# Router on un-normalised rows, with the bias, statistics and slot integers moved to other places in the queues

## What is computed

```python
x = x + xattn(layernorm(x), ctx)            # 16 heads of 16, softmax(q k^T / 4) v, then Wo and bo
xf = layernorm(x).reshape(-1, 256)
logits = xf @ router_w.T + router_b         # 32 experts
e = argmax(logits)
out = x + relu(relu(xf @ w1[e] + b1[e]) @ w2[e] + b2[e])
```

## Time and profile before

| | |
|---|---|
| median of three runs | 1132.77 us (1130.8 to 1137.42) |
| the profiled execution: time, span of its core | 1134.33 us, 1132.5 us |
| PE busy | 1050.1 us, 93% |
| DVE busy | 916.1 us, 81% |
| ACT busy | 825.7 us, 73% |
| POOL busy | 839.3 us, 74% |
| mean granted clock of PE | 0.973 of 2.4 GHz |

### The profile page before, as it was taken

One profiled execution on the slowest core, in us unless ns is written; L12 is line 12 of the kernel. 1 busy time (PEld: TensorE's weight loads), 2 busy tenths in 40 slices (PEclk: granted clock), 3 DMA queues, 4 the chain that ended last, 5 costly groups with the idle time before them and its releaser, 6 DMA issues.

```text
span 1132.5 us, 39071 instructions
## 1 busy us (share of the span) xinstructions
PE 1050.1 (93%) x15015; PEld 877.7 (77%) x15015; DVE 916.1 (81%) x2355; ACT 825.7 (73%) x1892; POOL 839.3 (74%) x1579
## 2 busy tenths in 40 slices
PE   5998999999999999999999999999998369998982
PEld 4887888878888888888888888888886258887872
DVE  4887788888888888888888888888887547776761
ACT  5776787878888888888888888888885236665651
POOL 5436688778878887888888878878866747777776
PEclk9999999999999999999999999999999679999997
DMA  7525222532222222323222222222210366666650
GB/s 234 186 60 130 77 78 77 125 105 77 77 78 82 82 86 78 90 82 104 83 83 77 77 78 77 78 77 78 72 53 22 109 190 200 208 207 210 202 150 12
DMA packets 91164, 120.38 MB, mean 106 GB/s; under 512 B 14105, under 2 KB 73892, under 8 KB 90790
## 3 DMA queue, kind: packets, MB, share of 16 engines
q1 hardware_dynamic: 77159, 84.04, 26.1%
q0 software_dynamic: 13824, 33.85, 8.3%
HBM read 60.61 MB, written 59.31 MB: 106 GB/s over the span
## 4 chain that ended last, share of the span: by engine, by line
PE 80%; DVE 5%; DMA 5%; POOL 4%; issue 3%; ACT 1%; SPq 0%; POOLq 0%; DVEq 0%; ACTq 0%
PE maxima L789 18%; PE pA L849 10%; PE sc L826 10%; PE sc L856 10%; PE sc L796 8%; PE sc L780 5%; PE sc L1036 4%; PE maxima L803 3%; PE maxima L1044 3%; POOL out L431 3%; PE sc L835 2%; DMA arena<-pages 2%; DMA out<-arena 2%; PE sc L1027 2%; PE pA L803 2%
## 5 line engine op out<-in xcount | busy, mean ns | idle before, releaser
L480 ACT ACTIVATE arena<-sc 128x512 f32<-128x512 f32 x512 | 264.4, 603 | 93.3 <-PE sc L835 93.3
L597 DVE TENSOR_REDUCE mx<-maxima 128x4 bf16<-128x512 f32 (+1 forms) x256 | 235.1, 919 | 5.2 <-PE maxima L803 4.0
L431 POOL DMA_INDIRECT out<-arena x160 | 157.6, 985 | 60.3 <-issue 30.8
L396 POOL DMA_INDIRECT pages<-row,slot_i x128 | 130.6, 1020 | 55.4 <-issue 53.4
L826 PE MATMUL sc<-qk 32*128 32x256 f32 x2048 | 152.1, 394 | 0.3 <-DVE xnT L617 0.3
L856 PE MATMUL sc<-wo_s,aT 128*128 128x256 f32 x512 | 132.5, 381 | 7.9 <-ACT arena L480 4.9
L849 PE MATMUL pA<-arena 128*32 128x128 f32 x4096 | 138.4, 276 | 0.0
L622 DVE STREAM_TRANSPOSE tr<-pA 128x512 f32<-128x512 f32 x128 | 90.7, 708 | 43.8 <-PE pA L849 43.4
L557 ACT ACTIVATE arena<-sc 128x256 f32<-128x256 f32 x160 | 61.5, 384 | 79.4 <-PE sc L1027 78.2
L849 PEld LDWEIGHTS pA<-arena 128*32 128x32 f32 x4096 | 107.1, 110 | 10.8 <-issue 5.0
L796 PE MATMUL sc<-wqkv,cHi 128*128 128x256 f32 x512 | 107.3, 302 | 0.0
(11 more groups left out here) (155 smaller groups left out, 2709.8 us busy)
## 6 DMA issues: line engine op xcount, KB each, us to landing
arena<-pages SPq DMA_DIRECT2D x160, 130.0 KB, 3.0
cT<-ctxT SPq DMA_DIRECT2D x64, 256.0 KB, 4.1
xs<-x_in SPq DMA_DIRECT2D x128, 128.0 KB, 3.4
pages<-empty SPq DMA_DIRECT2D x120, 130.0 KB, 3.5
pages<-empty SPq DMA_DIRECT2D x1, 5200.0 KB, 20.0
out<-arena POOLq DMA_INDIRECT x160
w2s<-w SPq DMA_DIRECT2D x1, 2080.0 KB
qk<-w SPq DMA_DIRECT2D x1, 2064.0 KB, 9.9
```

What stands on the lines that cost most here:

```text
L396: pool.indirect_dma_start(pages, bass.IndirectOffsetOnAxis(slot_i[:, q % 2, u:u + 1], 0), row[:, q % 4, u, :], None, bounds_check=last_slo ...
L431: pool.indirect_dma_start(out_rows, bass.IndirectOffsetOnAxis(pr[:, r, COL_TOKEN:COL_TOKEN + 1].bitcast(U32), 0), pr[:, r, 0:D], None, bou ...
L480: act.activation(pt[:, u % 2, g].rearrange("p i k -> p (i k)"), sc[g][:, :], ACT.Exp).then_inc(S["exp_out"], 1)
L597: dve.tensor_reduce(mx[:, :].rearrange("p (g h) -> p g h", h=32)[:, g:g + n, 0:4], src.rearrange("p (g h k) -> p g h k", g=n, h=4), AX.X, ...
```

## The change

The router is applied to the rows as they are. Its weights are centred in the set-up: a product of a constant 1/D matrix with the weights gives their means, and DVE subtracts these (`wr_c`). So the mean of a row drops out, and only its factor is missing; `logits_across` applies it as the per-token scale of four activations of 32 columns, and the router's bias is added by DVE as a new first operation of `best`. `norm2` and `xn2` go, and PE transposes `row` directly, waiting for the residual only. In the queues: on POOL `place(s-3)` stands ahead of `add_bo(s)`, which now waits for the normalise of the last unit of the block before; the slot integers are made by DVE, behind `slot_sum`; on DVE `stats1(.., (3,))` of a block moves from u=3 of one superstep to u=0 of the next; and PE makes seven products of 512 columns between the last slot integers and the first page. The set-up loses the transposed router bias. The diff:

```diff
--- before.py
+++ after.py
@@ -79,18 +79,18 @@
         cst = sb("cst", [C_ALL])
         wqkv = sb("wqkv", [3, 2, 2, D], F32R)
         wo_s = sb("wo_s", [2, D])
-        wr_s = sb("wr_s", [2, E])
+        wr_s, wr_c = sb("wr_s", [2, E]), sb("wr_c", [2, E])
         bq_s, bk_s = sb("bq_s", [2]), sb("bk_s", [2])
         bqm = sb("bqm", [2, 2])
         bv_s, bo_s, rb_s = sb("bv_s", [D]), sb("bo_s", [D]), sb("rb_s", [E])
         bvT = sb("bvT", [2, P])
-        rb4, rbp = sb("rb4", [QB, E]), sb("rbp", [1])
+        rb4 = sb("rb4", [QB, E])
         ident_b, tri_b, ones_b = sb("ident_b", [P], BF16), sb("tri_b", [P], BF16), sb("ones_b", [P], BF16)
         sel_b = sb("sel_b", [4, P], BF16)
         half = sb("half", [QB])
         xs = sb("xs", [4, QB, D])
         row = sb("row", [4, QB, ROW])
-        xn, xn2 = sb("xn", [QB, D]), sb("xn2", [QB, D])
+        xn, sq = sb("xn", [QB, D]), sb("sq", [2, D])
         xnT = sb("xnT", [2, 2, QB * P], F32R)
         xn2T = sb("xn2T", [2, QB * P])
         cT = sb("cT", [2, QB * P])
@@ -144,9 +144,9 @@
 
         names = """ld_c0 ld_c1 ld_cst ld_wk ld_wq ld_wv ld_b ld_wo ld_wr ld_w1 ld_w2 fill fill0 fill1 fill2 fill3
           pool_init dve_init cst_ready mask_ready wk_hi wq_hi wv_hi wk_lo wq_lo wv_lo w2_zero ex_init
-          bvT_done bvT_out bo_done bo_out rbT_done rbp_out rb4_out
+          bvT_done bvT_out bo_done bo_out wr_out rb4_out
           S_done T_done PV_done O_done V_done proj_done mxT_done xnT_done xn2T_done lg_done lgT_done rk_done
-          exp_out V_out proj_out xnT_out xn2T_out lgs_out rk_out xn_out xn2_out
+          exp_out V_out proj_out xnT_out xn2T_out lgs_out rk_out xn_out lb_out
           max_out mxT_out tr_out inv_out nrm_out aT_out x2_out sq_out stat1_out agg1_out xnTl_out
           lg_out top_out eq_out pick_out idx_out hot_out scan_out slot_out
           var1_out pow1_out mr1_out rstd1_out mean2_out sq2_out eps2_out var2_out pow2_out rstd2_out
@@ -352,7 +352,7 @@
                     pool.wait_ge(S["bo_out"], 1)
                 after(pool, "xn_out", 2, q, 1)
                 if q >= 1:
-                    after(pool, "nrm_out", 4, q - 1, 2)
+                    after(pool, "nrm_out", 4, q - 1, 3)
                 pool.tensor_tensor(xs[:, q % 4], xs[:, q % 4], bo_s[:, :].unsqueeze(1).to_broadcast([P, QB, D]),
                                    ALU.add).then_inc(S["xb_out"], 1)
 
@@ -379,12 +379,6 @@
                 pool.tensor_copy(row[:, q % 4, :, COL_EXPERT].bitcast(I32), expert[:, :]).then_inc(S["meta_out"], 1)
                 pool.tensor_scalar(tok[:, :], tok[:, :], float(QB * P), None, ALU.add).then_inc(S["tok_out"], 1)
 
-            def slots_as_integers(q):
-                if q >= 2:
-                    scattered(pool, q - 2)
-                after(pool, "slot_out", 1, q, 0)
-                pool.tensor_copy(slot_i[:, q % 2, :], slot[:, :]).then_inc(S["slot_int"], 1)
-
             def scatter(q):
                 if q == 0:
                     pool.wait_ge(S["fill"], 16)
@@ -405,10 +399,10 @@
             for s in range(-1, NQ + 3):
                 if live(s - 1):
                     rstd2(s - 1, 0)
+                if 0 <= s - 3 < LATE:
+                    place(pool, s - 3)
                 if live(s):
                     add_bo(s)
-                if 0 <= s - 3 < LATE:
-                    place(pool, s - 3)
                 if live(s + 2):
                     rstd1(s + 2)
                 if s >= 0 and live(s + 2):
@@ -418,7 +412,6 @@
                 if s >= 0 and live(s + 2):
                     split_low(s + 2)
                 if live(s - 3):
-                    slots_as_integers(s - 3)
                     scatter(s - 3)
                 if live(s - 2):
                     meta(s - 2)
@@ -449,19 +442,9 @@
                 if u % 2:
                     ins.then_inc(S["xn_out"], 1)
 
-            def norm2(q, u):
-                after(act, "rstd2_out", 2, q, u // 2)
-                if u == 0:
-                    after(act, "sq_out", 4, q, 3)
-                ins = act.activation(xn2[:, u, :], row[:, q % 4, u, 0:D], ACT.Identity,
-                                     scale=row[:, q % 4, u, COL_RSTD:COL_RSTD + 1],
-                                     bias=row[:, q % 4, u, COL_MEAN:COL_MEAN + 1])
-                if u % 2:
-                    ins.then_inc(S["xn2_out"], 1)
-
             def squares(q, u):
                 after(act, "x2_out", 4, q, u)
-                act.activation(xn2[:, u % 2, :], row[:, q % 4, u, 0:D], ACT.Square, scale=D ** -0.5,
+                act.activation(sq[:, u % 2, :], row[:, q % 4, u, 0:D], ACT.Square, scale=D ** -0.5,
                                accum_out=row[:, q % 4, u, COL_RSTD:COL_RSTD + 1]).then_inc(S["sq_out"], 1)
 
             def xnT_copy(q, h):
@@ -497,13 +480,17 @@
 
             def logits_copy(q):
                 after(act, "lg_done", 1, q, 0)
-                act.activation(lgs[:, :], sc[3][:, 0:P], ACT.Identity, bias=rbp[:, 0:1]).then_inc(S["lgs_out"], 1)
+                act.activation(lgs[:, :], sc[3][:, 0:P], ACT.Copy).then_inc(S["lgs_out"], 1)
 
             def logits_across(q):
                 after(act, "lgT_done", 1, q, 0)
                 if q >= 1:
                     after(act, "eq_out", 1, q - 1, 0)
-                act.activation(lg[:, :, :].rearrange("p u e -> p (u e)"), sc[3][:, 0:P], ACT.Copy).then_inc(S["lg_out"], 1)
+                after(act, "rstd2_out", 2, q, 1)
+                for u in range(QB):
+                    ins = act.activation(lg[:, u, :], sc[3][:, u * E:(u + 1) * E], ACT.Identity,
+                                         scale=row[:, q % 4, u, COL_RSTD:COL_RSTD + 1])
+                ins.then_inc(S["lg_out"], 1)
 
             def rank_copy(q):
                 after(act, "rk_done", 1, q, 0)
@@ -523,9 +510,6 @@
                     if u == 0 and live(s + 1) and s >= 0:
                         norm1(s + 1, 2)
                         norm1(s + 1, 3)
-                    if u in (1, 2) and live(s - 1):
-                        norm2(s - 1, 2 * u - 2)
-                        norm2(s - 1, 2 * u - 1)
                     if live(s):
                         exps(s, u)
                     q, n = chunk_of(s, u)
@@ -546,8 +530,6 @@
                     if u == 2 and live(s - 2):
                         rank_copy(s - 2)
                     if u == 3 and live(s - 1):
-                        if s == 1:
-                            act.wait_ge(S["rbp_out"], 1)
                         logits_copy(s - 1)
                     if live(q1):
                         squares(q1, u1)
@@ -573,7 +555,8 @@
             dve.memset(run[:, :, :], 0.0).then_inc(S["dve_init"], 1)
             dve.memset(zer[:, :], 0.0).then_inc(S["dve_init"], 1)
             dve.memset(ones_b[:, :], 1.0).then_inc(S["dve_init"], 1)
-            dve.wait_ge(S["dve_init"], 3)
+            dve.memset(tr[:, 0:P], 1.0 / D).then_inc(S["dve_init"], 1)
+            dve.wait_ge(S["dve_init"], 4)
 
             def own(name, value, ins):
                 ins.then_inc(S[name], 1)
@@ -637,6 +620,7 @@
 
             def best(q):
                 after(dve, "lg_out", 1, q, 0)
+                own("lb_out", q + 1, dve.tensor_tensor(lg[:, :, :], lg[:, :, :], rb4[:, :, :], ALU.add))
                 own("top_out", q + 1, dve.tensor_reduce(top[:, :], lg[:, :, :], AX.X, ALU.max))
                 dve.tensor_tensor(eq[:, :, :], lg[:, :, :], over_e(top), ALU.is_equal).then_inc(S["eq_out"], 1)
 
@@ -658,9 +642,11 @@
 
             def slot_sum(q):
                 after(dve, "own_slots", 1, q, 0)
-                if q >= 1:
-                    after(dve, "slot_int", 1, q - 1, 0)
                 dve.tensor_reduce(slot[:, :], t1[:, :, :], AX.X, ALU.add).then_inc(S["slot_out"], 1)
+                if q >= 2:
+                    scattered(dve, q - 2)
+                after(dve, "slot_out", 1, q, 0)
+                dve.tensor_copy(slot_i[:, q % 2, :], slot[:, :]).then_inc(S["slot_int"], 1)
 
             def low(w):
                 dve.wait_ge(S[("wq_hi", "wk_hi", "wv_hi")[w]], 1)
@@ -677,12 +663,12 @@
             def biases():
                 dve.wait_ge(S["bvT_done"], 1)
                 dve.tensor_copy(bvT[:, :, :].rearrange("p c t -> p (c t)"), sc[1][:, 0:2 * P]).then_inc(S["bvT_out"], 1)
-                dve.wait_ge(S["rbT_done"], 1)
-                dve.tensor_copy(rbp[:, :], sc[3][:, 0:1]).then_inc(S["rbp_out"], 1)
 
             def output_bias():
                 dve.wait_ge(S["bo_done"], 1)
                 dve.tensor_tensor(bo_s[:, :], bo_s[:, :], sc[1][:, 0:D], ALU.add).then_inc(S["bo_out"], 1)
+                dve.tensor_tensor(wr_c[:, :, :], wr_s[:, :, :], sc[1][:, D:D + E].unsqueeze(1).to_broadcast([P, 2, E]),
+                                  ALU.subtract).then_inc(S["wr_out"], 1)
 
             stats1(0, (0, 1, 2, 3))
             dve.wait_ge(S["ld_cst"], 16)
@@ -714,6 +700,8 @@
                         slot_sum(s - 3)
                     if live(qn):
```

(25 more changed lines are left out.)

## The result

The changed kernel takes 1223.0 us (median of 6 runs, 1219.5 to 1223.9), the kernel before 1134.7 us (6 runs): the ratio is 1.077, 95% interval 1.075 to 1.080. It is slower by 88 us. The forecast was 1184.2 us with a range of 1158 to 1212: the direction and the mechanism came as forecast, the size didn't, and the time lies above the range, near rival B (1220 us). The profiled execution took 1223.92 us, with a span of 1222.1 us.

What follows compares the result with a forecast made beforehand. PE, closely followed by DVE, bounds the first stage, POOL's scatters the second. The profiled span 1132.5 + 53 (hold) + 0.8 (normalise) + 0 - 2.5 (matmuls) + 0.2 (set-up) = 1184.0 us; forecast median 1184.2, range 1158 to 1212.

Steps and rivals of the forecast that it cites:

- rival B: Loop: the hold comes and PE's clock falls too, 1.3 us more a superstep; +90 us, 1220 us; chance 0.07.
- Statistics and router's bias: Loop, u=1: moved statistics delay POOL's L368, which holds the new sum of `best`; +1.9 us a superstep, +53 us (34 to 67).
- The clock: Loop, behind PE's wait: no term in the sum; a fall of the clock appeared only in rival B.
- DVE has room: Tail of u=0: 0.77 us of DVE idle time takes the moved statistics and 0.24 us of slot integers.
- Scan: DVE, u=3: the scan no longer meets POOL's L356, 0.8 us less of DVE; gain 0.1 us a superstep (0 to 0.4).
- The held normalise: DVE, u=1: L364, if first, holds the normalise up to 0.8 us, already counted; supersteps 0 and 1 pay +0.8 us.
- The norm removed: Stage one: four activations a superstep leave ScalarE, none on PE's path; cost and gain 0.
- Seam: Between the stages: last `rstd2` +0.6 us, superstep 31 +0.3, slot casts and wait -1; sum 0 (-1 to +1).
- Seven matmuls: PE, ahead of the first page: they end 1 to 2 us before it is ready; -2.5 us (-3 to +4).
- Rival A: Loop: no hold, `best` and L368 don't meet; 1127 to 1136 us; chance 0.15.

Runs made afterwards that it cites:

- experiments 1: Changed kernel with the first half of the next block's statistics put back behind the tail of u=3; 1147.4 us, 1.011 times the kernel before.
- experiment 2: Kernel before with only the statistics moved from the tail of u=3 to u=0 of the following superstep; 1165.0 us, ratio 1.027.
- experiment 4: Changed kernel with both splits ahead of the first root in POOL's queue, statistics still at u=0; 1147.9 us, ratio 1.011.
- 6: Changed kernel without the sum of the router's bias, which is left out of the logits; 1175.9 us in one profiled run.
- Experiments 7 to 9: Changed kernel with statistics back, splits first and bias sum earlier, plus 3, 6 and 5 idle DVE reductions per superstep; 1162.1, 1217.5 and 1178.7 us.
- 5: Changed kernel with both splits first on POOL and the statistics behind `xnT_lo` instead of ahead of it; 1137.6 us in one profiled run.
- experiment 3: Kernel before with only `place` put ahead of `add_bo` in POOL's queue; 1130.6 us, ratio 0.9965.
- Experiment 11: Changed kernel with statistics back, splits first, bias sum earlier, and 11 matmuls instead of 7 ahead of the pages; 1127.6 us, ratio 0.9961.
- 10: Changed kernel with statistics back, splits first on POOL and the bias sum ahead of the residual in the same tail; 1129.8 us, ratio 0.9974.

## Why the prediction was right in kind and wrong in size

- **Statistics and router's bias: right.** Unit 3 grows by 2.00 us without a fall, as forecast (2.0), and experiments 1, 2, 4 and 6 show the cause: take away the overlap with the square (4) and the hold goes, shorten it (1) and it shrinks, put another two-input operation there (2, 6) and that one is held. The superstep of 28.7 us against a forecast of 28.5 is 28 x 2.1 = 59 us of the 90.7.
- **The clock: the step that failed.** The sum has no term for it: the stall of 2 us was priced by its length alone, and the clock was left to rival B, with a chance of 0.07, on the evidence that a unit held for 0.4 us showed nothing more. But that unit was 0.33 us longer, and the forecast was of one 2.0 us longer. Experiments 7 to 9 show that waits of PE up to 1.19 us cost only themselves, and one of 1.51 us brings the clock down in most supersteps. From "nothing happens at 0.3" I inferred "nothing happens at 2". B priced it at 1.3 us in all 28 supersteps, a figure that came from no row; it is 1.6 us in 21: 34 us, which is the whole miss of 39 us but for 5. That B's 1220 us lies so near the result is luck in part: 28 x 1.3 and 21 x 1.6 are nearly the same.
- **"DVE has room": wrong.** I put the moved statistics and the slot integers into the 0.77 us of idle time ahead of `tr` and counted nothing. The instruction between them and that idle time, `xnT_lo`, has a reader of its own, PE's scores. It starts 0.9 us later in its unit, PE lost 0.24 us a superstep by it (of 0.34 in all), and experiments 4 and 5 show it. These 28 x 0.24 = 7 us, less the 3 us that the scan gave beyond its 0.1, are most of the 5 us that the clock leaves. The idle time before an instruction is room only if nobody waits for what stands between.
- **Scan: right in size, low by a bit.** Unit 1 is 0.21 us shorter (forecast 0.1, bounds 0 and 0.4). In the kernel before alone (experiment 3) 0.13 of the 0.20 us are lost to the next hold.
- **The held normalise: wrong way round.** L611 at 541.45 came 0.04 us ahead of L364 and took 0.42 us; L364 took 1.28 us instead of 1.04 beside it. I had let L364 go first, and where it does (experiment 2), the normalise pays 0.76 us. The 0.24 us delayed the square, which is where the forecast for L368 is short by 0.2.
- **The norm removed: right**, no gain: 47 us less of ScalarE are not on the path.
- **Seam: right.** From the last `rstd2` to the last scatter are 19.5 us, before 20.4: the forecast 1 us. From the last transpose of the maxima to the first out-scatter there is +0.06 us.
- **Seven matmuls: wrong.** Forecast -2.5 us with a gap of 1 to 2 us behind them; the gap was 4.3 us, the clock had fallen again, and they gave nothing. Experiment 11 has the gap that I had assumed and wins 1.5 us, so that this size was too large as well.
- **Rival A** did not come. The order on POOL alone (experiment 4) takes back 75 of the 88 us, to 1147.9; with the order on DVE set right as well it is 1137.6 (5) and 1129.8 us (10), the last inside A's 1127 to 1136. So nearly all of the loss was one of order and not of work.

The terms of the loop, 59 and 34 us, are 2 us more than the 90.7 measured. Among supersteps 2, 3 and 7 every kernel has one or two with a long stall (33.7 us in superstep 3 before, 35.2 after), and these vary by that much.

## What to carry over

When an instruction is moved to another place in a queue, follow its result as well as its time: here 0.6 us of statistics, moved, cost 31 us, and 88 with the new sum, because a long operation of the other engine was queued behind their reader and slid over the first two-input operation of DVE. Put the long operation of the second engine ahead of whatever waits for a moved result, and ask for each neighbour that is pushed back who reads it. And price a stall of PE twice, once for its length and once for the clock behind it: a small stall that shows no fall says nothing of a stall of several times its length.
